# One head's 272 columns and a 512-column piece issued in turn, and four matmuls instead of five ahead of a weighted sum

## The reference

```
# layer 0
h = max(layernorm(x), 0)
x = x + adj @ (h @ W0) + b0
# layer 1: 8 heads of 256 columns
h = max(layernorm(x), 0)
feat_proj = h @ fc_w + fc_b                  # per head
logits = q + k^T                             # q, k = feat_proj @ q_w, feat_proj @ k_w
masked = leaky_relu(logits + (1 - adj) * -1e9, 0.01)
out = softmax(masked) @ feat_proj            # per head
x = x + sigmoid(concat(out) @ fp_w + fp_b + h)
```

## Time and profile before

| | |
|---|---|
| median of 3 runs | 1397.38 us (1395.92 to 1397.95) |
| the profiled execution | 1396.24 us, its span 1394.4 us |
| PE busy | 1382.7 us, 99% of the span, 9624 matmuls |
| DVE, POOL, ACT busy | 1284.0, 1125.7, 1095.2 us |
| DMA | 123.13 MB, mean 88 GB/s |
| chain that ended last | PE 91%, POOL 3%, issue 2%, DVE 2% |

### The profile page before, as it was taken

The page is one execution under the profiler, slowest core; times in us unless marked ns, Lnnn a source line. Parts: engine busy times, 40 slices in busy tenths (PEclk is TensorE's granted clock), DMA queues, the critical chain, the costliest instruction groups (busy, mean ns, idle before and its releaser), DMA issues.

```text
span 1394.4 us, 32661 instructions
## 1 busy us (share of the span) xinstructions
PE 1382.7 (99%) x9624; PEld 1274.3 (91%) x9624; DVE 1284.0 (92%) x4536; ACT 1095.2 (79%) x3428; POOL 1125.7 (81%) x1291
## 2 busy tenths in 40 slices
PE   8999999999999999999999999999999999999998
PEld 7889999999999999999999899999999999999997
DVE  7998999999999999999999899999999999999996
ACT  4778787787787887887877778878878778778776
POOL 4788888888788788788888887887888888888874
PEclk9999999999999999999999999999999999999999
DMA  6313133132232232331331322323312213223111
GB/s 227 100 71 107 56 105 101 57 106 85 73 106 74 85 106 69 90 106 54 105 105 54 106 76 83 106 71 87 106 57 102 105 54 106 84 74 106 58 57 54
DMA packets 43246, 123.13 MB, mean 88 GB/s; under 512 B 5969, under 2 KB 9681, under 8 KB 43217
## 3 DMA queue, kind: packets, MB, share of 16 engines
q1 hardware_dynamic: 42928, 122.77, 28.2%
q10 hardware_dynamic: 288, 0.01, 0.0%
HBM read 105.46 MB, written 17.30 MB: 88 GB/s over the span
## 4 chain that ended last, share of the span: by engine, by line
PE 91%; POOL 3%; issue 2%; DVE 2%; ACT 1%; DMA 1%; SPq 0%; POOLq 0%; DVEq 0%
PE gbank L405 44%; PE ybank L405 23%; PE bank L405 9%; PE tbank L532 7%; PE bank L450 4%; PE bank L480 2%; POOL att L1650 1%; POOL att L1643 1%; DMA late<-fc_wT_dram 1%; DVE att L907 1%; PE gbank L425 1%; PE bank L458 0%; ACT att L1326 0%; POOL feats L1659 0%; DVE att L914 0%
## 5 line engine op out<-in xcount | busy, mean ns | idle before, releaser
L1326 ACT ACTIVATE att<-att 128x128 f32<-128x128 f32 x1024 | 398.9, 393 | 145.1 <-DVE att L914 143.4
L1643 POOL TENSOR_TENSOR att<-late,t_pos 128x512 f32<-128x512 f32 x256 | 333.4, 1303 | 131.1 <-PE tbank L532 74.5
L405 PE MATMUL gbank<-m_hi,hT_lo 128*128 128x512 f32 (+1 forms) x1024 | 383.6, 375 | 0.6 <-DVE g_lo L890 0.6
L405 PE MATMUL gbank<-m_hi,hT_hi 128*128 128x512 f32 (+1 forms) x1024 | 382.5, 373 | 0.0
L405 PE MATMUL gbank<-m_lo,hT_hi 128*128 128x512 f32 (+1 forms) x1024 | 373.3, 367 | 0.0
L1650 POOL TENSOR_TENSOR att<-att,rinv 128x512 f32<-128x512 f32 x256 | 291.3, 1138 | 86.0 <-DVE rinv L919 85.7
L890 DVE TENSOR_TENSOR g_lo<-gbank,g_hi 128x512 fp32r<-128x512 f32 x448 | 302.8, 680 | 12.9 <-ACT g_hi L1319 6.8
L907 DVE TENSOR_SCALAR_CACHE_REDUCE att<-att,kq_sb 128x128 f32<-128x128 f32 x1024 | 287.2, 341 | 5.2 <-POOL att L1643 4.8
L1319 ACT ACTIVATE g_hi<-gbank 128x512 fp32r<-128x512 f32 x448 | 255.4, 586 | 5.2 <-PE gbank L405 4.8
L405 PE MATMUL ybank<-g_hi,pT_lo 128*128 128x256 f32 x889 | 246.6, 277 | 0.1
L405 PE MATMUL ybank<-g_hi,pT_hi 128*128 128x256 f32 x889 | 246.3, 277 | 0.0
(11 more groups left out here) (123 smaller groups left out, 2885.8 us busy)
## 6 DMA issues: line engine op xcount, KB each, us to landing
late<-key_rows SPq DMA_DIRECT2D x128, 512.0 KB, 6.2
g_in<-graph_dram SPq DMA_DIRECT2D x64, 512.0 KB, 3.4
out_dram<-ends SPq DMA_DIRECT2D x63, 256.0 KB, 6.0
att<-fc_wT_dram SPq DMA_DIRECT2D x4, 256.0 KB, 5.6
late<-fp_w_dram SPq DMA_DIRECT2D x4, 256.0 KB, 5.3
ends<-fp_w_dram SPq DMA_DIRECT2D x2, 512.0 KB, 7.8
late<-fc_wT_dram SPq DMA_DIRECT2D x2, 512.0 KB, 9.6
key_rows<-rows SPq DMA_DIRECT2D x64, 8.0 KB, 1.4
```

What stands on the lines that cost most here:

```text
L405: mm = pe.matmul(out_ap, w, m, start=first and n == 0, stop=last and n == len(terms) - 1)
L1326: e = act.activation(a[:, s], a[:, s], ACT.Exp, scale=-1.0, bias=a[:, CH + h:CH + h + 1], accum_out=esum[j][c][:, h:h + 1])
L1643: gp.tensor_tensor(a, keys[q][:, j, c * HC:(c + 1) * HC, :], t_pos[q][:, j, :].unsqueeze(1).broadcast_to([P, HC, P]), ALU.add)\
```

## The change

TensorE's order and, in one place, VectorE's order are changed; no instruction is added or left out. In every turn, and likewise in `finish()`:

- One matmul instead of two of piece `A1` stands ahead of `attend(i - 1, ..., 0, 1)`, so with the three of `B0` there are four matmuls of 512 columns ahead of graph 0's sum over heads 4 to 7, and five instead of four behind the transposes of `h`.
- Graph 0's last head and piece `A0` are issued in turn, one matmul of each, six pairs, in two banks that are both open. Piece `A0` no longer stands behind graph 1's last head.
- On VectorE, in the loop alone, `inverse(i, 0, 0)` and `leaky(i, 0, 1)` move ahead of the work on graph 0's last head.

```diff
-            def last_head(p, q, j):
-                bank = here if j == 0 else ring_free(THERE, p)
-                folded(p)
-                split(bank[:, 0:WIDE],
-                      [((hT_hi[q][:, dt, j, :], hT_lo[q][:, dt, j, :]), (n_hi[:, dt, 0:WIDE], n_lo[:, dt, 0:WIDE]))
-                       for dt in range(DT)]).then_inc(pe_g[LAST[j]], 1)
+            def last_terms(q, j, out_ap, part):
+                return split(out_ap,
+                             [((hT_hi[q][:, dt, j, :], hT_lo[q][:, dt, j, :]), (n_hi[:, dt, 0:WIDE], n_lo[:, dt, 0:WIDE]))
+                              for dt in range(DT)], part=part)
+
+            def last_head(p, q, j):
+                bank = here if j == 0 else ring_free(THERE, p)
+                folded(p)
+                last_terms(q, j, bank[:, 0:WIDE], slice(None)).then_inc(pe_g[LAST[j]], 1)
+
+            def last_head_and_piece(p, q, i, r):
+                bank = ring_free(A0, i)
+                for n in range(TERMS):
+                    head = last_terms(q, 0, here[:, 0:WIDE], slice(n, n + 1))
+                    if n == TERMS - 1:
+                        head.then_inc(pe_g[HERE], 1)
+                    mm = piece_terms(r, A0, bank[:], slice(n, n + 1))
+                mm.then_inc(pe_g[A0], 1)
...
             def step(i, q):
                 project_part(i - 1, (q + 2) % U, B0, 3, 6)
-                project_part(i, q, A1, 0, 2)
+                project_part(i, q, A1, 0, 1)
                 attend(i - 1, (q + 2) % U, 0, 1)
                 transpose_h(i + 1, (q + 1) % U)
-                project_part(i, q, A1, 2, 6)
+                project_part(i, q, A1, 1, 6)
                 transpose_p(i - 1, 1, 1)
                 project(i, q, A2)
                 h_ready(i + 1)
-                last_head(i + 1, (q + 1) % U, 0)
+                last_head_and_piece(i + 1, (q + 1) % U, i, q)
                 last_head(i + 1, (q + 1) % U, 1)
-                project(i, q, A0)
                 project_part(i, q, B1, 0, 1)
                 attend(i - 1, (q + 2) % U, 1, 0)
                 attend(i - 1, (q + 2) % U, 1, 1)
...
                 pT_low(i - 1, 1, 1)
+                inverse(i, 0, 0)
+                leaky(i, 0, 1)
                 keys_queries(i + 1, (q + 1) % U, 0)
                 last_low(i + 1, (q + 1) % U, 0)
-                inverse(i, 0, 0)
-                leaky(i, 0, 1)
                 keys_queries(i + 1, (q + 1) % U, 1)
```

More of the change, by code:

```diff
@@ L698, in finish @@
                 project_part(60, 0, B0, 3, 6)
-                project_part(61, 1, A1, 0, 2)
+                project_part(61, 1, A1, 0, 1)
                 attend(60, 0, 0, 1)
                 transpose_h(62, 2)
-                project_part(61, 1, A1, 2, 6)
+                project_part(61, 1, A1, 1, 6)
                 transpose_p(60, 1, 1)
@@ L705, in finish @@
                 h_ready(62)
-                last_head(62, 2, 0)
+                last_head_and_piece(62, 2, 61, 1)
                 last_head(62, 2, 1)
-                project(61, 1, A0)
                 project_part(61, 1, B1, 0, 1)
@@ L723, in finish @@
                 project_part(61, 1, B0, 3, 6)
-                project_part(62, 2, A1, 0, 2)
+                project_part(62, 2, A1, 0, 1)
                 attend(61, 1, 0, 1)
                 transpose_h(63, 0)
-                project_part(62, 2, A1, 2, 6)
+                project_part(62, 2, A1, 1, 6)
                 transpose_p(61, 1, 1)
@@ L730, in finish @@
                 h_ready(63)
-                last_head(63, 0, 0)
+                last_head_and_piece(63, 0, 62, 2)
                 last_head(63, 0, 1)
-                project(62, 2, A0)
                 project_part(62, 2, B1, 0, 1)
@@ L747, in finish @@
                 project_part(62, 2, B0, 3, 6)
-                project_part(63, 0, A1, 0, 2)
+                project_part(63, 0, A1, 0, 1)
                 attend(62, 2, 0, 1)
-                project_part(63, 0, A1, 2, 6)
+                project_part(63, 0, A1, 1, 6)
                 transpose_p(62, 1, 1)
```

## The result

The changed kernel takes 1399.28 us (median of 19 runs, 1398.34 to 1401.06), the kernel before beside it 1396.42 (19 runs): ratio 1.0018, 95% interval 1.0011 to 1.0025. It is slower by 2.5 us by the ratio (1.5 to 3.5) and by 2.9 by the medians. The forecast was 1393.3, faster by 4.1, so the sign is wrong, though the time lies inside the range.

What follows compares the result with a forecast made beforehand. The prediction took TensorE's pace of starting one matmul after another as the bound. Gains of 3.2 and 0.9 us, other terms 0, took 1397.38 to 1393.3 us; own range 1391 to 1395, 8-in-10 range 1389.7 to 1400.5.

Steps and rivals of the forecast that it cites:

- The second sums of graph 0: Graph 0's heads 4 to 7: twelve matmuls at 1.36 us instead of 1.42 behind four 512s, 3.2 us gained.
- The moved 512: A1's matmul moved behind the transposes of h: 0 to +6 ns each, at most +0.35 us, taken as 0.
- The six pairs: Graph 0's last head in turn with A0: 0.357 us a pair, no change, bounds 3.2 us either side.
- graph 1's last head: Its six 272s now follow a 512 of 394 ns and get cheaper: 0.9 us gained.
- The last 512 ahead of graph 1's sums: One 512 instead of seven between the 272s and graph 1's sums still has 394, sums stay cheap: 0.
- the first rival: Graph 1's 24 sum matmuls turn dear behind the lone 512: 6.5 us more; chance 0.15.
- The first rival's sum: Whole-kernel time if graph 1's sums turn dear, with the other terms kept: 1399.8 us.
- The order is worth nothing: Second rival: TensorE's reordering changes no time, 1397.4 us; chance 0.22 together with pairs dearer by 9 ns.
- The waits: Graph 0's last head completes later, but covers, the shortest 1.2 us, hold: no new wait in TensorE.
- The sum: Whole kernel: 3.2 + 0.9 = 4.1 us less, median 1393.3 us.

Runs made afterwards that it cites:

- run 7: Kernel before with six 512s instead of five ahead of graph 0's sum over heads 4 to 7: 1397.52 us, against 1398.63 beside it.
- run 8: Kernel before with seven 512s instead of five ahead of graph 0's sum over heads 4 to 7: 1396.18 us, against 1398.63 beside it.
- run 1: Kernel before with only four 512s instead of five ahead of graph 0's sum over heads 4 to 7: ratio 0.9986, 1395.59 against 1397.07 us.
- run 3: Kernel before with VectorE's new order alone: ratio 0.9986, 1395.52 us.
- run 6: Changed kernel with three 512s of B1 instead of one between graph 1's last head and graph 1's sums: 1407.29 us, against 1398.63 for before.
- run 13: Changed kernel with graph 1's last head ahead of the six pairs and no 512 between pairs and graph 1's sums: 1399.75 us, against 1399.70 for before.
- run 12: Changed kernel with graph 1's last head ahead of the six pairs instead of behind them: 1402.31 us, against a median of 1395.92 for before.
- run 2: Changed kernel with A1 split as before, so five 512s ahead of graph 0's sum over heads 4 to 7: ratio 1.0042 to before, 1403.7 us.

## Why the prediction was wrong

- *The second sums of graph 0*, 3.2 us gained: right. 1.37 us and 276 ns in the changed kernel; the twelve sums took 0.052 us less. Runs 7 and 8 bear out the rule behind it, for most turns.
- *The moved 512*, at 0 with +0.35 us at most: too small. The rest of `A1`, the transposes and `A2` took 0.018 us more a turn together, 1.1 us in all, in the changed kernel and in run 1 alike (medians over the turns).
- *The six pairs*, nothing, and *graph 1's last head*, 0.9 gained: the gain did not come. From the start of the first 272 to that of graph 1's sums it is 3.125 us before and 3.133 in the changed kernel (medians): 0.5 us lost in all instead of 0.9 gained. In run 1, without pairs, it is 3.107: the 272s are at the lower price already there, where the last 512 of `A2` has 394 and no longer the 392 of the earlier trace rows. With the second rhythm of graph 1's head that gain is gone. The six pairs by themselves took 699.87 - 697.73 = 2.14 us, the 6 x 0.357 of the prediction.
- *The last 512 ahead of graph 1's sums*, at 0: this is the step that failed. "One is 7 less two full turns of the cycle" supposed that any run of 272s hands over the same state. Twelve of them do in 54 of 56 turns; six behind the pairs do in one of 56. In 53 turns they keep a rhythm of 124 and 129 ns, the 512 gets 396 instead of 394, and the 24 sums cost 2.83 us instead of 2.72: 0.11 x 59 = 6.5 us, the price that the first rival named. I gave that rival 0.15 with "a single 512 is in no row" as its ground. The ground was good and the chance too small: the rows of two other paces of the 272s had shown that their state varies, and two turns of the kernel before hold the very case.
- *The first rival's sum*, 2.4 us more than before, is close to the 2.5 measured, and that is in part luck: it still had the 0.9 us gained and left out the 1.1 and 0.5 us lost, and VectorE's order, which it left out too, makes up for most of that if it is worth 2.0 here.
- *The order is worth nothing*: it is worth something (runs 1, 7 and 8). The formula that the prediction takes from the Trainium skill, "TensorE: Matmul & The Clock Gate", section "Back-to-back issue gap", is given there for an isolated matmul, and for a stream the section says that weight load and matmul together set the spacing. Neither has a place for what stands ahead, on which these runs show 1.37 or 1.42 us to hang for the same twelve matmuls.
- *The waits*: right. The covers held; ScalarE's exponential waited 59.9 us in all for VectorE instead of 143.4. The edit of VectorE's order, which the sum left out, was worth 2.0 us in the kernel before (0.7 to 3.2, run 3). What it is worth with the pairs no run shows.
- *The sum.* The undisturbed turn is longer by 0.08 us (21.206 to 21.286), 4.7 us in 59 turns: 3.1 gained, 6.3 to 6.5 lost to the sums of graph 1, 1.1 and 0.5 to the rest. If VectorE's 2.0 us hold here too, that makes +2.7, and +2.5 was measured.

What stays open is what the state is. No run tells why behind the pairs, or without them behind some pauses of TensorE, the 272s fall into the second rhythm, nor which resource sets the 394, 388, 392 cycle. The count rule predicts most turns; it does not explain.

## What to carry to other kernels

Where one engine's issue pace is the bound, look at what one and the same instruction costs in different places: a 4% difference between equal runs, with nothing waiting, is a lead. Such a pace may hang on what stands ahead, so every reordering moves it elsewhere too; before adding up gains, list each run whose predecessors change, and price it at the dear value unless a row shows exactly its new predecessors. And test the parts of a change apart: here two of three edits helped, and the third cost more than both gave. And look through all the turns of a trace and not only at one: here the rare turns of the kernel before already showed the case that decided.

## What the runs showed of the hardware

- A run of 256-column matmuls started each 113 ns behind the last (276 ns recorded) or each 118 (279 to 280), with equal shapes, operands and a granted clock of 1.00, and kept the pace for 24 matmuls. Behind transposes, four or seven 512s gave the first in most turns (52 of 56 in run 1, 53 of 56 in run 8), five, six or eight the second (before, runs 6, 7, 13). Four gave the second in 19 of 56 turns of run 12, seven in 36 of 55 of run 2.
- 512-column matmuls started 226, 229 and 232 ns apart in turn (388, 392, 394 recorded), or, behind 272-column ones of 287 and 291 ns in turn, some 234 apart all the time (396 to 398), and the 256s behind those went at the slower pace.
- Issuing 272- and 512-column matmuls in turn, into two banks, cost 0.357 us a pair, as much as in runs.
- A load of 512 KB for which GpSimd waited 3.19 us instead of 1.0 reached TensorE as a delay of some 0.7 us in one matmul's start (0.93 us behind the last instead of 0.23), two engines further on.
